# One transformer block on one core: the counts of a threshold search, the slot lists of the router, and the order of the opening rows

## The reference, cut to what matters

```
h = layernorm(x) * (1 + ca) + sa                    # ca, sa, ga ... from silu(c) @ wmod, per image
q, k, v = h @ Wq.T + bq, h @ Wk.T + bk, h @ Wv.T + bv
k = causal_conv(k, ssm_k_kernel) + ssm_k_D * k      # by FFT along the tokens, 512 taps
kv = outer products of k and v within each of 32 heads (8 x 8)
y = causal_conv(kv, ssm_kernel) + D * kv
y = sum over one index of q * y;  x = x + ga * (y @ Wo.T + bo)
h = layernorm(x) * (1 + cb) + sb
probs = softmax(h @ Wr)                             # 8 experts, the best 2 of each token
for e in range(8):                                  # each expert takes its 1280 best tokens
    vals, idx = top_k(where(e is among the token's 2, prob, -inf), 1280)
    y[idx] += gate * (relu(h[idx] @ W1[e]) @ W2[e])
x = x + gb * y
```

## Time and profile before

| | |
|---|---|
| median of 3 runs | 1213.57 us (1211.91 to 1213.63) |
| the profiled execution | 1209.35 us, span 1207.5 us |
| TensorE busy | 1129.0 us, 93% of the span |
| VectorE busy | 816.3 us, 68% |
| ScalarE busy | 420.4 us, 35% |
| GpSimd busy | 544.8 us, 45% |
| mean granted clock of TensorE | 0.945 |

### The profile page before, as it was taken

How to read it: one execution, slowest core, us unless ns; L and a number is a source line. 1 busy time by engine, 2 the same in 40 slices (tenths; PEclk the granted TensorE clock), 3 DMA queues, 4 the chain that set the end, 5 groups by cost and what they waited for, 6 DMA issues and landing times.

```text
span 1207.5 us, 17088 instructions
## 1 busy us (share of the span) xinstructions
PE 1129.0 (93%) x5810; PEld 980.5 (81%) x5810; DVE 816.3 (68%) x1549; ACT 420.4 (35%) x762; POOL 544.8 (45%) x403
## 2 busy tenths in 40 slices
PE   8998999999999999999985558999999999999996
PEld 5877888888888888887874447989898989899996
DVE  5587999589999999998476785444444444445442
ACT  5321122323223333231572202344353434444432
POOL 3220000377777777772000032666565657565723
PEclk9998999999999999999885558999999999999998
DMA  7110022433001111102441212754444353534322
GB/s 266 36 35 12 1 45 52 137 122 97 27 31 33 33 33 33 33 22 70 140 145 37 91 55 56 201 141 88 118 85 122 79 127 87 131 67 83 57 41 26
DMA packets 73985, 93.35 MB, mean 77 GB/s; under 512 B 5924, under 2 KB 61988, under 8 KB 73944
## 3 DMA queue, kind: packets, MB, share of 16 engines
q1 hardware_dynamic: 55928, 60.96, 16.3%
q0 software_dynamic: 18016, 31.86, 13.6%
HBM read 65.29 MB, written 23.31 MB: 73 GB/s over the span
## 4 chain that ended last, share of the span: by engine, by line
PE 73%; issue 13%; DVE 7%; ACT 2%; DMA 2%; POOL 2%; SPq 0%; DVEq 0%; POOLq 0%; ACTq 0%
PE ps L1459 27%; PE ps L1600 18%; PE ps L1616 12%; PE ps L1617 6%; PE ps L1487 2%; PE ps L1370 2%; DVE arena L1155 1%; PE ps L1582 1%; DMA qkv<-in_w 1%; DVE qkv L821 1%; PE ps L1562 1%; DVE arena_rounded L821 1%; PE ps L1545 1%; PE ps L1510 1%; ACT qkv L732 1%
## 5 line engine op out<-in xcount | busy, mean ns | idle before, releaser
L1600 PE MATMUL ps<-arena_rounded,w_high 128*128 128x384 f32 (+1 forms) x768 | 210.5, 355 | 2.1 <-DVE arena_rounded L821 2.1
L580 POOL TENSOR_TENSOR kv_low<-arena,kv_high 128x512 fp32r<-128x512 f32 x128 | 185.7, 1479 | 41.1 <-ACT kv_high L632 41.1
L1459 PE MATMUL ps<-kv_high,toep_high 128*128 128x512 f32 (+1 forms) x512 | 193.1, 377 | 1.0 <-POOL kv_low L580 1.0
L1459 PE MATMUL ps<-kv_low,toep_high 128*128 128x512 f32 (+1 forms) x512 | 193.1, 377 | 0.0
L1459 PE MATMUL ps<-kv_high,toep_low 128*128 128x512 f32 (+1 forms) x512 | 192.4, 376 | 0.0
L1272 DVE SCALAR_TENSOR_TENSOR hidden_low<-ps,hidden_high 128x384 fp32r<-128x384 f32 (+1 forms) x192 | 115.6, 602 | 98.9 <-ACT hidden_high L790 98.5
L604 POOL DMA_INDIRECT out<-arena x80 | 126.3, 1579 | 103.7 <-DVE arena L821 96.0
L593 POOL DMA_INDIRECT qkv<-row_scratch,arena x80 | 82.9, 1036 | 184.0 <-DVE arena L1226 158.0
L1600 PEld LDWEIGHTS ps<-arena_rounded,w_high 128*128 128x128 f32 x768 | 139.9, 189 | 13.2 <-issue 2.5
L790 ACT ACTIVATE hidden_high<-ps 128x384 fp32r<-128x384 f32 (+1 forms) x192 | 101.3, 528 | 125.6 <-PE ps L1600 125.6
L821 DVE TENSOR_TENSOR arena<-qkv 128x512 f32 (+1 forms) x128 | 133.3, 1099 | 7.2 <-DMA qkv<-arena 7.0
(11 more groups left out here) (198 smaller groups left out, 1971.9 us busy)
## 6 DMA issues: line engine op xcount, KB each, us to landing
arena<-ssm_scratch SPq DMA_DIRECT2D x32, 320.0 KB, 3.1
qkv<-in_w SPq DMA_DIRECT2D x16, 512.0 KB, 5.2
qkv<-in_w SPq DMA_DIRECT2D x8, 1024.0 KB, 10.7
arena<-in_u SPq DMA_DIRECT2D x7, 1024.0 KB, 6.2
row_scratch<-qkv SPq DMA_DIRECT2D x4, 1056.0 KB, 4.6
qkv<-arena SPq DMA_DIRECT2D x32, 128.0 KB, 2.4
row_scratch<-arena SPq DMA_DIRECT2D x4, 1024.0 KB, 6.4
out<-qkv SPq DMA_DIRECT2D x4, 1024.0 KB, 9.3
```

What stands on the lines that cost most here:

```text
L580: nc.gpsimd.tensor_tensor(kv_parts[s][1][:, quarter], kv_flat[s][:, quarter], kv_parts[s][0][:, quarter].bitcast(F32), ALU.subtract).then_ ...
L1459: last = mm(ps[:, 4 * s + g, (lo - 2 * g) * B * 64:BANK], toep_parts[s][a][:, o * P:(o + 1) * P], kv_parts[s][x][:, src], start=n == 0 and ...
L1600: last = mm(ps[:, f % 4, 0:width], w1_parts[q][a][:, dc * F + f * P:dc * F + (f + 1) * P], xeT_parts[x][dc][:, 0:width], start=dc == 0 and ...
```

## The change

Three parts. In the search, the counts become four columns of rounded type, the sum over the 16 partitions a matmul of rounded operands with a rounded copy of the ones (made by ScalarE before the closing of the attention), the test multiplies with the candidate, and the accepted digit is the largest of the three products; the table `digit_unit` and its load go away. In the first slot lists the codes become the stationary side and the lanes the moving one; the result is transposed, so ScalarE copies it to SBUF and TensorE transposes it back (`mark_rows_turned`), before VectorE reads it. In the opening, forward 0 moves ahead of tile 3 of image 2 and forward 1 behind that image, the transposes of image 1 move behind tile 5 of image 0 (and VectorE's modulation of them with it), the transposes of image 3 wait for the copied spectrum of unit 0, and VectorE's and ScalarE's programs take unit 0 in earlier places. The definitions of the new semaphores and the count of loaded constants (7 for 8) are left out here.

```diff
         bo_gated = region(T0 + 3072, B * D).rearrange("p (b n) -> p b n", b=B)
+        group_ones_r = arena_r[:, KK0 + 3968:KK0 + 3968 + P]
...
+
+        turned_marks = [region(R2 + 768 + 1024 * i, P) for i in range(2)]
...
-        count = sb("count", [P, 3])
+        count = sb("count", [P, 4], F32R)
...
@@ -679,7 +681,6 @@
                                      ACT.Copy, scale=1.0 / HALF).then_inc(kk_copied, 1)
             h_high(2)
             normalize_x(3)
-            h_high(3)
...
-            for unit in range(4):
+            act.wait_ge(taps_ready, 1)
+            spec_out(0)
+            h_high(3)
+            for unit in range(1, 4):
                 spec_out(unit)
             for unit in range(UNITS):
...
+            act.wait_ge(consts_in, 16 * 7)
+            copy(group_ones_r, group_ones[:]).then_inc(ones_ready, 1)
             y_turned(0)
...
             weights_high(0, 0, range(PIECES))
+            for k, width in enumerate((BLOCKS, REST)):
+                act.wait_ge(mark_psum, k + 1)
+                copy(turned_marks[k][0:width, :], ps[0:width, 4 + k, 0:P]).then_inc(mark_copied, 1)
...
                 link(last)
+                dve.sem_inc(taps_ready, 1)
...
-                    if b == 2 and t == TB - 1:
-                        dve.wait_ge(consts_in, 16 * 8)
+                    if b == 2 and t == 3:
+                        dve.wait_ge(consts_in, 16 * 7)
                         joined_spectrum(dve, link, 0)
-                    if t == TB // 2 and b + 1 < B:
+                    if t == (6 if b == 0 else TB // 2):
                         h_rows(b + 1)
+                    if b == 2 and t == 5:
+                        turned_half(link)
+                    if b == 2 and t == 6:
+                        real_products(link, 0)
+                    if b == 2 and t == 7:
+                        real_difference(link)
...
-            turned_half(link)
-            real_products(link, 0)
-            real_difference(link)
             imaginary_products(link, 0)
             imaginary_sum(link)
             folded_product(dve, link, 0)
-            for unit, t in ((1, 0), (2, TB // 2)):
-                qkv_rows(B - 1, t)
-                joined_spectrum(dve, link, unit)
-                qkv_rows(B - 1, t + 1)
-                turned_half(link)
-                qkv_rows(B - 1, t + 2)
-                real_products(link, unit)
-                qkv_rows(B - 1, t + 3)
-                real_difference(link)
-                imaginary_products(link, unit)
-                imaginary_sum(link)
-                if unit == 1:
-                    dve.wait_ge(hT_low, 4 * B)
-                    dve.wait_ge(mod_out, 16)
-                folded_product(dve, link, unit)
+            qkv_rows(B - 1, 0)
+            qkv_rows(B - 1, 1)
+            joined_spectrum(dve, link, 1)
+            qkv_rows(B - 1, 2)
+            turned_half(link)
+            qkv_rows(B - 1, 3)
+            real_products(link, 1)
+            real_difference(link)
+            imaginary_products(link, 1)
+            imaginary_sum(link)
+            qkv_rows(B - 1, 4)
+            dve.wait_ge(hT_low, 4 * B)
+            dve.wait_ge(mod_out, 16)
+            folded_product(dve, link, 1)
+            qkv_rows(B - 1, 5)
+            qkv_rows(B - 1, 6)
+            joined_spectrum(dve, link, 2)
+            qkv_rows(B - 1, 7)
+            turned_half(link)
+            real_products(link, 2)
+            real_difference(link)
+            imaginary_products(link, 2)
+            imaginary_sum(link)
+            folded_product(dve, link, 2)
...
+            nc.vector.tensor_copy(count[:, 3:4], eps[:])
...
                     tt(base[:], theta[:].to_broadcast([P, 3]), digit_int[:, bass.ds(n * 3 + 3, 3)], ALU.bitwise_or)
                     dve.wait_ge(count_psum, n + 1)
 
-                    link(nc.vector.tensor_scalar(reached[:], ps[:, 1, 0:3], float(CAP), None, ALU.is_ge, ALU.add, accum_out=digit[:]))
-                    link(nc.vector.tensor_scalar(accepted[:], digit[:], digit_unit[:, bass.ds(n, 1)], None, ALU.mult))
+                    link(nc.vector.scalar_tensor_tensor(reached[:], ps[:, 1, 0:3], float(CAP), cand[:].bitcast(F32),
+                                                        ALU.is_ge, ALU.mult))
+                    link(nc.vector.tensor_reduce(accepted[:].bitcast(F32), reached[:], AX.X, ALU.max))
...
-            row_numbers(ps[:, 4, 0:BLOCKS], 0, BLOCKS)
+            row_numbers(ps[:, 4, 2 * P:2 * P + BLOCKS], 0, BLOCKS)
             mark_codes(code_of[0], 0, BLOCKS, LISTS)
             for c in range(4):
...
-            nc.vector.tensor_copy(code_rest[:, 0:REST], ps[:, 5, 0:REST]).then_inc(rest_copied, 1)
+            nc.vector.tensor_copy(code_rest[:, 0:REST], ps[:, 5, 2 * P:2 * P + REST]).then_inc(rest_copied, 1)
...
                 if b == 3:
-                    pe.wait_ge(modT_ready, 4)
-                    pe.wait_ge(mod_read, 1)
+                    pe.wait_ge(spec_ready, JP + 4)
...
                 pe.wait_ge(qkv_ready, TB * (b + 1))
-                pe.wait_ge(h_full_ready, 4 * B)
+                pe.wait_ge(h_full_ready, 4 * (B - 1 if unit == 0 else B))
...
-            for b in range(B):
-                if b == 0:
-                    qkv_products(0, range(1))
-                    h_transposes(0, (2, 3))
-                    qkv_products(0, range(1, TB // 2))
-                else:
-                    qkv_products(b, range(TB // 2))
-                if b + 1 < B:
-                    h_transposes(b + 1)
-                if b == B - 2:
-                    qkv_products(b, range(TB // 2, TB - 2))
-                    forward(0)
-                    qkv_products(b, range(TB - 2, TB))
-                    forward(1)
-                    continue
-                if b == B - 1:
-                    forward(2)
-                qkv_products(b, range(TB // 2, TB))
-                if b == 0:
-                    taps_spectrum()
-                if b == 1:
-                    late_modulation()
+            qkv_products(0, range(1))
+            h_transposes(0, (2, 3))
+            qkv_products(0, range(1, TB // 2))
+            qkv_products(0, range(TB // 2, 6))
+            h_transposes(1)
+            qkv_products(0, range(6, TB))
+            taps_spectrum()
+            qkv_products(1, range(TB // 2))
+            h_transposes(2)
+            qkv_products(1, range(TB // 2, TB))
+            late_modulation()
+            qkv_products(2, range(3))
+            pe.wait_ge(modT_ready, 4)
+            pe.wait_ge(mod_read, 1)
+            forward(0)
+            qkv_products(2, range(3, TB // 2))
+            h_transposes(3)
+            qkv_products(2, range(TB // 2, TB))
+            forward(1)
+            qkv_products(3, range(TB // 2))
+            forward(2)
+            qkv_products(3, range(TB // 2, TB))
             forward(3)
...
+            pe.wait_ge(ones_ready, 1)
             for i in range(BITS // 2):
                 pe.wait_ge(count_ready, i + 1)
-                mm(ps[:, 1, 0:3], group_ones[:], count[:], start=True, stop=True).then_inc(count_psum, 1)
+                mm(ps[:, 1, 0:4], group_ones_r, count[:], start=True, stop=True).then_inc(count_psum, 1)
                 rows_back(i + 1)
             pe.wait_ge(count_ready, BITS // 2 + 1)
-            mm(ps[:, 1, 0:1], group_ones[:], count[:, 0:1], start=True, stop=True).then_inc(count_psum, 1)
+            mm(ps[:, 1, 0:4], group_ones_r, count[:], start=True, stop=True).then_inc(count_psum, 1)
...
-            def of_first(t):
-                return lane_first[:, t]
+            def mark_rows_turned(k, bank, codes, width, by_chunk):
+                for t in range(TILES):
+                    if by_chunk and t % 8 == 0:
+                        pe.wait_ge(lanes_ready, t // 8 + 1)
+                    end = mm(ps[0:width, bank, 0:P], codes[:, t], lane_first[:, t], start=t == 0, stop=t == TILES - 1)
+                end.then_inc(mark_psum, 1)
+                pe.wait_ge(mark_copied, k + 1)
+                transpose(ps[:, bank, 2 * P:2 * P + width], turned_marks[k][0:width, :], ident[0:width, 0:width]).then_inc(code_psum, 1)
...
             pe.wait_ge(codes_ready, 1)
-            mark_rows(4, code_0, of_first, BLOCKS, True)
+            mark_rows_turned(0, 4, code_0, BLOCKS, True)
             pe.wait_ge(codes_ready, 2)
-            mark_rows(5, code_of[0], of_first, REST, False)
+            mark_rows_turned(1, 5, code_of[0], REST, False)
```

More of the change, by code:

```diff
@@ L93, in constants @@
         "digit_int": np.tile(np.append(4 ** np.arange(BITS // 2 - 1, -1, -1)[:, None] * np.arange(1, 4), [0, 0, 0]).astype(np.int32), (P, 1)),
-        "digit_unit": np.tile((4.0 ** np.arange(BITS // 2 - 1, -1, -1)).astype(np.float32), (P, 1)),
         "expert_id": np.tile(np.arange(E, dtype=np.float32), (P, 1)),
@@ L254, in adaln_block @@
         digit_int = sb("digit_int_sb", [P, 3 * BITS // 2 + 3], I32)
-        digit_unit = sb("digit_unit_sb", [P, BITS // 2])
```

(11 more changed lines are left out.)

## The result

| | before | after |
|---|---|---|
| median | 1213.54 us (4 runs, 1211.91 to 1213.63) | 1197.05 us (4 runs, 1196.24 to 1198.37) |
| the profiled execution | 1209.35 us, span 1207.5 | 1197.35 us, span 1195.6 |
| mean granted clock there | 0.945 | 0.952 |

The medians lie 16.5 us apart. The ratio, 0.9875 with a 95% interval of 0.9861 to 0.9889, comes to 15.2 us (13.5 to 16.9); 14.8 were forecast. The two profiled executions are only 12.0 us apart; where the rest comes from is the first thing to settle, since the prediction had carried the 4.2 us between profile and median over as if it were fixed.

What follows compares the result with a forecast made beforehand. TensorE's matmuls bound 73% of the span; in the opening VectorE and TensorE were nearly equal, in the search one dependent chain. -7.3 - 6.2 - 1.3 = -14.8 us, from 1213.57 to 1198.8 us; range 1194.5 to 1206.5.

Steps and rivals of the forecast that it cites:

- Opening, -7.3: Opening: forward 0 and the join of spectrum 0 come earlier, VectorE ends last, inverse 7 starts at 214.5: -7.3 us.
- 1 us for the new wait on a tile of image 3: Opening, VectorE's chain: 1 us added for waiting on a tile of image 3, within the 131.6 us.
- Rival 1: Opening: TensorE's clock falls in the new 2.4 us hole, costing about 3 us: 1201.8; chance 0.10.
- TensorE below full clock between 85 and 125 us: Opening: sign that would show the forecast wrong, TensorE's clock not full between 85 and 125 us.
- Search, -6.2: Search: fifteen rounds each 0.40 us shorter (count matmul 0.24, VectorE's pair 0.16), last count 0.24: -6.2 us.
- the search 4.1: Search: if a second matmul pass cost only 107 ns, the search would lose 4.1 us, the sum 1201.0 us.
- Lists, -1.3: First slot lists: row numbers come 1.3 us earlier, limited by VectorE's weight remainders: -1.3 us, bounds -1.3 to 0.
- rival 4: First slot lists: narrow rounded streams take 0.43 us per 128 columns, giving 1214.9, with a late clock 1217; chance 0.05.
- the term for the clock: Start of the experts: the earlier start shifts TensorE's clock rise either way; 2 us both ways, with other low stretches.
- Profile to median: Whole kernel: profiled execution 1209.35 us, 4.2 below the median 1213.57; that difference carried over from 1194.6 to 1198.8 us.

Runs made afterwards that it cites:

- after again: The changed kernel, with no further edit, timed and profiled once more: median 1197.88 us, ratio 0.9874 to the kernel before.
- rows apart: Changed kernel with image 3's rows on VectorE in two pairs and unit 0's turned half after GpSimd's last remainders: 0.9850, again 0.9846 (1194.50 us), against the kernel before.

## Why the prediction was right, step by step

**Opening, -7.3.** Forward 0 at 76.6 (measured 76.21), the join at 84.3 (84.04), VectorE last: right. Inverse 7 was to start at 214.5 and came at 215.99 (215.49 in the other profile). The failing term is "1 us for the new wait on a tile of image 3": it measured 1.6 (0.46 and 1.14; 0.15 and 0.79 in "after again"), and 1.05 for the half-turn beside GpSimd was not in the sum at all. The Trainium skill, "SBUF — State Buffer", section "SBUF: two separate sides", says that a VectorE operation with two SBUF inputs and a GpSimd operation that reads SBUF lock each other out for a whole instruction. The trace agrees: the half-turn, whose two large inputs lie in SBUF, takes 1.79 us when it starts in the middle of the subtraction, 0.83 at its end, 0.74 beyond it, while VectorE's bias rows, which read one input from PSUM, keep their 0.94 to 0.96 us beside the same subtractions. Against the first profile the opening therefore gave 5.7 at the first gated sum, within the bounds but 1.6 under the forecast; over the means of the executions it gave 7.0, because the old opening loses 0.8 and 1.7 us to two falls of the clock, neither of which that one profile showed.

**Rival 1** rested on "holes of 2.25 and 1.97 us passed without it". They had, in one execution; in the next, both were followed by a fall. In the new order the clock did fall behind the hole, in one of two profiles of the changed kernel and in both other profiles with this opening, but at a price of 0.3 to 0.7 us, not 3. So the condition of the rival came true, and with it a sign that the prediction had listed as wrong, TensorE below full clock between 85 and 125 us; its price was the error, because VectorE covers most of the fall.

**Search, -6.2.** Measured 6.2. The single matmul took 0.37, not 0.347, and gave 3.3 where the working had 3.8; the pair gave 2.7 instead of 2.4. By the load time of the Trainium skill ("TensorE: Matmul & The Clock Gate", section "LDWEIGHTS (loading the stationary operand)") the second pass would be worth 0.107 us and the search 4.1, by the prediction's estimate. The measurement decides against it here: leaving the second pass out gave 0.22 us a round.

**Lists, -1.3.** Right up to the experts: 1.4, VectorE the limit. A matmul that loads 10 columns and streams 128 takes at most some 0.12 us (32 in 3.97 with waits for lanes between them), so rival 4 falls. But no gain shows at the end: the term for the clock, "up to some us in either direction", was taken as chance, and with the new lists it went one way in four of five executions. Whether the lists are the cause is open.

**Profile to median.** The 4.2 us were carried over as a constant. In the second profile of before (1213.74) they were two falls and one longer wait, and the change removes the two falls: by that profile the opening gave 8.1, and span to span 16.3. So the total of 14.8, 1.7 short of the medians and 0.4 of the ratio, came out so close partly by luck: this error and the lists' probable one have opposite signs.

## What to carry over

Before trusting a profile that lies below the kernel's timed runs, profile the kernel a second time: a wait that left the clock alone in one execution can cost more in the next (with its fall, 2.25 us became 3.1 and 1.97 became 3.7). In a chain that two engines share, look for work of one that sits between the other's tiles and waits for a third; pulling such work apart gave more here than its own waits. And a gain in front of the clock's rise is to be checked at the end of the kernel: here the 1.4 us of the lists could be seen up to the experts, and no longer at the end.

## What the hardware showed unexpectedly

The clock: identical waits (2.25 us before the transposes, 2.15 before tile 6) were followed by a fall in some executions and not in others, with the same program. What a fall of 3.4 us costs depends on the place: 0.8 us behind the transposes, 1.7 behind forward 0, 0.3 to 0.7 where VectorE is the bound. From the search to the start of the first expert TensorE is at half clock; but in all five profiles with the new lists it was granted full clock for a moment there (695.7 to 699.1 us in the changed kernel, about the end of the first lists; in three of the five once more about the end of the second), and in none of nine with the old ones, whose matmuls keep it busy for longer. Why stays open, and so does whether the order of "rows apart" with the old lists would win the pair of falls back; that was not run.
